# Third block's attention: query and key parts split on GpSimd, a running sum of the chunks, one total a group

## The chip, the cores and the metric

One core of a Trainium2 chip runs the whole program. The metric is device time in microseconds: the median of the timed runs. The engines are TensorE (PE in the profile; PEld are its weight loads), VectorE (DVE), ScalarE (ACT), GpSimd (POOL) and SyncE (SP), which here only issues DMAs. Each engine works through its own list of instructions in order; semaphores tie the lists together.

## The reference

Four transformer-like blocks run one after the other. The change touches the attention of the third:

```python
def _L2_xattn_ref(x, latents, attention_mask, ...):      # x: 64 context rows, latents: 512 rows, batch 4
    h = jnp.concatenate([x, latents], axis=1)            # 576 keys
    q = (latents @ q_w + q_b).reshape(b, k_len, NH, DH)  # 16 heads of 32
    kv = (h @ kv_w + kv_b).reshape(b, p + k_len, NH, DH, 2)
    kmat, v = (kv[..., 0], kv[..., 1])
    attn = jnp.einsum('bkhd,bnhd->bhkn', q, kmat) / DH
    attn = jnp.where(full_mask[:, None, None, :], attn, -jnp.inf)
    attn = jax.nn.softmax(attn.astype(jnp.float32), axis=-1).astype(q.dtype)
    attn_out = jnp.einsum('bhkn,bnhd->bkhd', attn, v).reshape(b, k_len, H)
    attn_out = attn_out @ out_w + out_b + residual
```

## The kernel before

`l2_attention_stage` handles 16 groups (`ALL`), each four heads of one of four batches; `turns(g)` is true for the second group of a batch but the last. Five chunks of keys (`CHUNKS`: four of 128 and one of 64 context keys) make up the 576.

For a group, TensorE projects the queries (`project_q`, four blocks of 512 columns) and keys (`project_k`, eight of 288). ScalarE copies them out with their bias (`take_projections`). VectorE splits each value into a rounded high part and the rest (`split`, two casts and two subtracts), so that logits can be computed in the fast float32r format. SP copies the parts with 24 DMAs into a stacked operand of each head (`load_stack`: `q_stack`, `k_stack`, six DMAs a head, double buffered over groups; a mask row goes first in the first two groups of a batch). TensorE then computes plain logits for 16 tiles (`logits`, four heads by four row blocks, each as two matmuls of 288 columns into `slot`), VectorE takes their row maximum (`maximum`, L1250), and four tiles of maxima are turned (`turn_tops`) and copied by ScalarE into the stack (`take_tops`). Now the turned logits (`logits_across`, L1093, keys on partitions) come out with the maximum already subtracted; ScalarE takes their exponential into `weighed`, a ring of three chunks (`exps`, L1204). `mix` multiplies the chunk with the values; ones matmuls (L1112, L1115) add the chunks up into `totals`. GpSimd adds chunks 0 and 1, and 2 and 3, so that TensorE needs one total of each pair and one of chunk 4. VectorE divides (`normalise`: reciprocal L1264, then a product) and, at the end of a batch, the output is projected (`project_out`, L1057).

The groups are staggered by hand. TensorE's list for group g holds, for chunks 0 to 3 and heads 0 to 3, a turned product of g and a logits tile of g+1 (a "step" below, numbered 0 to 15), with a mix of the previous chunk behind every four; then the last chunk's four products with the query projection of g+3 between them, the turning of the maxima of g+1, the last mixes and totals, and the key projection of g+3. After a batch's last group come the values of the next batch and the output projection. In its loop VectorE takes 16 maxima of g+1, normalises g, then splits g+3; SP loads the stack of g+2 as soon as the turned products of g are done with its buffer. A logits tile may run two ahead of its maximum, a turned product two ahead of its exponential.

## Time and profile before

| what | value |
|---|---|
| median of 3 runs | 3097.59 us (3094.41 to 3097.8) |
| the profiled execution | 3090.94 us, its span 3089.1 us |
| PE busy in the span | 2789.1 us (90%) |
| PE weight loads | 1982.5 us (64%) |
| DVE busy | 1472.4 us (48%) |
| ACT busy | 839.5 us (27%) |
| POOL busy | 349.2 us (11%) |
| the third block's attention | from 1354.2 us to about 2022 us |
| GpSimd's pair adds in it (L986) | 32, 145.5 us |
| the maxima (L1250) | 256, 183.1 us |
| the exponentials (L1204) | 320, 184.5 us |

Busy times are shares of the whole span, over stages with different limits; what an edit is worth here is read from the stretch of this attention alone. A matmul record's end is modelled, since matmuls are pipelined: the distance between starts tells more than the duration. A time in brackets is how long the engine was idle before the row, with what released it. The profile leaves the block's digit out of buffer names: `l_slot` is this stage's `l2_slot`. A matmul of plain float32 is recorded as two, one of float32r as one.

### The profile page before, as it was taken

The page shows a single profiled execution, that of the slowest core. Times are in us where ns is not written, and L with a number is a line of the kernel's source. Part 1 is how long each engine was busy: PE and PEld are TensorE (multiplying, and loading weights), DVE is VectorE, ACT ScalarE, POOL GpSimd, SP SyncE. Part 2 cuts the span into 40 slices and gives each one's busy share as a digit, 9 for nine tenths or more (in the row PEclk, how much of TensorE's full clock was granted, in tenths as well). Part 3 has the DMA queues.
Part 4 walks back from the last instruction along what each step waited for, and adds up shares of the span by engine and source line. Part 5 has one row for each costly group of instructions (what it writes and reads, how often), then busy time and mean ns, then how long its engine had stood idle before and what let it go on. Part 6 is the DMA issues. An engine that isn't in the chain of part 4 may idle for free. (4 is left out here: it accounts for less than half of the span.)

```text
span 3089.1 us, 30932 instructions
## 1 busy us (share of the span) xinstructions
PE 2789.1 (90%) x11800; PEld 1982.5 (64%) x11800; DVE 1472.4 (48%) x2117; ACT 839.5 (27%) x1580; POOL 349.2 (11%) x178
## 2 busy tenths in 40 slices
PE   6999979999969999988999999869999788779999
PEld 4777656777758888744445454348888544468887
DVE  3564474455575343135545454455343545374443
ACT  4233314332331111213435242431111122241110
POOL 2000002000012000012313122312000300040000
PEclk9999989999979999978999999879999899989999
DMA  3111011101010000202121211130000101110001
GB/s 121 55 55 54 1 60 56 55 1 55 0 60 28 14 14 1 109 23 49 44 58 44 57 44 53 27 126 28 14 14 1 62 28 62 45 61 28 28 0 55
DMA packets 60095, 130.64 MB, mean 42 GB/s; under 512 B 30673, under 2 KB 30802, under 8 KB 49234
## 3 DMA queue, kind: packets, MB, share of 16 engines
q1 hardware_dynamic: 43218, 128.61, 12.3%
q10 hardware_dynamic: 16768, 0.53, 0.3%
q8 instruction: 74, 1.21, 0.2%
q14 instruction: 35, 0.29, 0.0%
HBM read 83.03 MB, written 8.45 MB: 30 GB/s over the span
## 5 line engine op out<-in xcount | busy, mean ns | idle before, releaser
L1204 ACT ACTIVATE l_weighed<-l_across 128x512 f32<-128x512 f32 (+1 forms) x320 | 184.5, 595 | 245.8 <-PE l_across L1093 240.8
L1250 DVE TENSOR_REDUCE l_top<-l_slot 128x1 f32<-128x576 f32 x256 | 183.1, 753 | 51.7 <-PE l_slot L1076 46.9
L986 POOL TENSOR_TENSOR l_paired<-l_weighed 128x2048 f32<-128x2048 f32 x32 | 145.5, 4546 | 464.8 <-ACT l_weighed L1204 380.9
L1076 PE MATMUL l_slot<-l_k_stack,l_q_stack 97*128 97x288 f32 x512 | 140.1, 361 | 34.2 <-DVE l_top L1250 20.9
L1093 PE MATMUL l_across<-l_q_stack,l_k_stack 99*128 99x512 f32 (+1 forms) x320 | 165.9, 522 | 3.9 <-ACT l_weighed L1204 3.7
L1076 PEld LDWEIGHTS l_slot<-l_k_stack,l_q_stack 97*128 97x128 f32 x512 | 100.8, 220 | 78.7 <-DVE l_top L1250 48.4
L1264 DVE RECIPROCAL l_inverse<-l_totals 128x512 f32<-128x512 f32 x16 | 53.7, 3357 | 158.6 <-PE l_totals L1115 158.6
L475 PE MATMUL l0b_wide<-l0b_key_map,l0b_norm 128*128 128x260 f32 x512 | 118.7, 385 | 9.3 <-DVE l0b_soft L630 7.2
L475 PE MATMUL l0a_wide<-l0a_key_map,l0a_norm 128*128 128x260 f32 x512 | 118.7, 385 | 9.3 <-DVE l0a_soft L630 7.2
L1755 ACT ACTIVATE l2m_hidden<-l2m_up,columns 128x512 f32<-128x512 f32 x64 | 44.2, 691 | 270.5 <-PE l2m_up L131 264.3
L1755 ACT ACTIVATE l0m_hidden<-l0m_up,columns 128x512 f32<-128x512 f32 x64 | 44.1, 691 | 269.7 <-PE l0m_up L131 262.6
L1755 ACT ACTIVATE l3m_hidden<-l3m_up,columns 128x512 f32<-128x512 f32 x64 | 44.1, 691 | 268.9 <-PE l3m_up L131 261.8
L475 PEld LDWEIGHTS l0b_wide<-l0b_key_map,l0b_norm 128*128 128x128 f32 x512 | 95.6, 190 | 27.6 <-DVE l0b_soft L630 9.8
L475 PEld LDWEIGHTS l0a_wide<-l0a_key_map,l0a_norm 128*128 128x128 f32 x512 | 95.6, 190 | 27.6 <-DVE l0a_soft L630 9.8
L1093 PEld LDWEIGHTS l_across<-l_q_stack,l_k_stack 99*128 99x128 f32 (+1 forms) x320 | 63.1, 199 | 73.8 <-issue 35.9
L129 PE MATMUL l0m_up<-l0m_norm_hi,l0m_w1h 128*128 128x512 f32 x256 | 101.6, 397 | 0.7 <-POOL l0m_w1l L1662 0.7
L129 PE MATMUL l3m_up<-l3m_norm_hi,l3m_w1h 128*128 128x512 f32 x256 | 101.0, 395 | 1.1 <-POOL l3m_w1l L1662 0.7
L129 PE MATMUL l2m_up<-l2m_norm_hi,l2m_w1h 128*128 128x512 f32 x256 | 101.2, 395 | 0.7 <-POOL l2m_w1l L1662 0.7
L130 PE MATMUL l0m_up<-l0m_norm_lo,l0m_w1h 128*128 128x512 f32 x256 | 101.0, 395 | 0.0
L131 PE MATMUL l0m_up<-l0m_norm_hi,l0m_w1l 128*128 128x512 f32 x256 | 100.6, 393 | 0.0
L130 PE MATMUL l2m_up<-l2m_norm_lo,l2m_w1h 128*128 128x512 f32 x256 | 100.6, 393 | 0.0
L131 PE MATMUL l2m_up<-l2m_norm_hi,l2m_w1l 128*128 128x512 f32 x256 | 100.5, 392 | 0.0
(391 smaller groups left out, 6240.9 us busy)
## 6 DMA issues: line engine op xcount, KB each, us to landing
l_k_stack<-l_k_parts SPq DMA_DIRECT2D x192, 72.0 KB, 2.0
l_q_stack<-l_q_parts SPq DMA_DIRECT2D x192, 64.0 KB, 2.0
l0m_raw<-in_weights SPq DMA_DIRECT2D x8, 1024.0 KB, 4.8
l2m_raw<-in_weights SPq DMA_DIRECT2D x8, 1024.0 KB, 6.4
l3m_raw<-in_weights SPq DMA_DIRECT2D x8, 1024.0 KB, 4.8
x<-in_x SPq DMA_DIRECT2D x4, 1024.0 KB, 8.9
l0a_wk<-in_weights SPq DMA_DIRECT2D x4, 1024.0 KB, 5.4
l0a_wv<-in_weights SPq DMA_DIRECT2D x4, 1024.0 KB, 7.3
```

Source lines behind the costliest of these rows:

```text
L129: pe.matmul(out, lh, rh, start=start, stop=False)
L130: pe.matmul(out, lh, rl, start=False, stop=False)
L131: return pe.matmul(out, ll, rh, start=False, stop=stop)
L475: last = pe.matmul(wide[:, j, 0:W], norm[:, k, at:at + P], key_map[:, k, b, :, :].rearrange("p h c -> p (h c)"), start=k == 0, stop=k == K ...
L986: pool.tensor_tensor(paired[:, :, :], weighed[:, first % RING, :, :], weighed[:, (first + 1) % RING, :, :], ALU.add)\
L1076: last = pe.matmul(slot[:, 2 * (i % 2) + half, 0:HALF], q_stack[0:ROW + 1, g % 2, j, t * P:(t + 1) * P], k_stack[0:ROW + 1, g % 2, j, half ...
L1093: pe.matmul(across[0:height(c), use % 2, :], k_stack[0:LAST, g % 2, j, keys_of(c)], q_stack[0:LAST, g % 2, j, :], start=True, stop=True).t ...
L1204: act.activation(weighed[0:height(c), (CHUNKS * g + c) % RING, j, :], across[0:height(c), use % 2, :], ACT.Exp)\
L1250: dve.tensor_reduce(top[:, i % TPB, i // TPB:i // TPB + 1], slot[:, 2 * (i % 2):2 * (i % 2) + 2, 0:HALF], AX.XY, ALU.max, negate=True).the ...
L1264: dve.reciprocal(inverse[:, :], totals[:, :]).then_inc(s["inverse_ready"], 1)
L1755: act.activation(hidden[:, i % 2, :], up[:, m, :], activation, bias=n.col(bias, f * KT + m))\
```

## The change

- The logits tile is one matmul of 512 columns; the 64 context columns of a head's four row blocks go as four short matmuls into a bank of their own (`ctx_slot`), with one maximum for all four (`ctx_top`), and `split_tops` first takes the smaller of the two negated maxima.
- The key projection is split into `project_k0` (512 columns) and `project_k1` (64). All blocks of `project_q`, `project_k0` and `project_k1` of group g+3 are dealt out between the steps by a table (`EXTRA`) and share one new bank, `work`. ScalarE's copies move in between its exponentials.
- From group 2 on, the split of g+2 runs on GpSimd, between its second and third add of group g; the parts have one buffer instead of two, and `projected` two instead of one.
- GpSimd keeps a running sum of all five chunks (`add_chunk`, four adds a group). TensorE has one `total` a group, in the next group behind its chunk 0, and for a batch's last group behind the next batch's values. The exponentials wait for the adds that read their buffer.
- The reciprocal is cut into four quarters (`invert`), taken with the product at places 5 to 9 of the next group's maxima, or behind the values at the end of a batch.
- The turning of the next batch's input (`turn_next`) moves to the steps of chunk 0; mixes 0 and 1 stand together behind chunk 2's steps.

```diff
+        VALUE_BANK = (0, 1, 2, 0, 1)
+        OUT_BANK = (2, 0, 1, 2)
+        EXTRA = (((0, 1, 2, 3), (6, 7, 8, 9), (13, 14, 16, 17)), ((4, 5, 6, 7), (9, 10, 11, 12), (16, 17, 18, 19)))
+
+        def bank_of(g, piece):
+
+            if g == 0:
+                return (work[:, :], slot_bank[0], slot_bank[1])[piece]
+            if g == 1:
+                return (slot_bank[2], work[:, :], slot_bank[0])[piece]
+            return work[:, :]
...
+            def add_chunk(g, c):
+                at, tall = CHUNKS * g + c, height(c)
+                pool.wait_ge(s["across_read"], across_use(g, c, 3) + 1)
+                if c == 1 and g:
+                    pool.wait_ge(s["totals_done"], g)
+                if c > 1:
+                    pool.wait_ge(s["chunk_summed"], (CHUNKS - 1) * g + c - 1)
+                so_far = summed[0:tall, :, :] if c > 1 else weighed[0:tall, (at - 1) % RING, :, :]
+                pool.tensor_tensor(summed[0:tall, :, :], so_far, weighed[0:tall, at % RING, :, :], ALU.add)\
+                    .then_inc(s["chunk_summed"], 1)
+
+            def split(g):
+                q, k = projected[:, g % 2, 0, 0:S], projected[:, g % 2, 1, :]
+                pool.wait_ge(s["k1_out"], g + 1)
+                for j in range(4):
+                    pool.wait_ge(stack_loaded[(g - 1) % 2][j], loaded(g - 1))
+                pool.tensor_copy(q_parts[:, 0, :], q)
+                pool.tensor_copy(k_parts[:, 0, :], k).then_inc(s["parts_high"], 1)
+                pool.wait_ge(s["parts_high"], g + 1)
+                pool.tensor_tensor(q_parts[:, 1, :], q, q_parts[:, 0, :].bitcast(F32), ALU.subtract)
+                pool.tensor_tensor(k_parts[:, 1, :], k, k_parts[:, 0, :].bitcast(F32), ALU.subtract).then_inc(s["parts_ready"], 1)
 
             for g in range(ALL):
                 b = g // GROUPS
-                add_pair(g, 0)
+                add_chunk(g, 1)
+                add_chunk(g, 2)
+                if g + 2 < ALL:
+                    split(g + 2)
                 if turns(g):
-                    pool.wait_ge(s["k_done"], GROUPS * (b + 1))
+                    pool.wait_ge(s["k1_done"], GROUPS * (b + 1))
                     pool.tensor_copy(source[:, :, S:KEYS], n.ctx_f[:, :, (b + 1) * C:(b + 2) * C]).then_inc(s["ctx_ready"], 1)
-                add_pair(g, 1)
+                add_chunk(g, 3)
+                add_chunk(g, 4)
...
+            def project_extra(g, step):
+                at_q, at_k0, at_k1 = EXTRA[g >= 3 and turns(g - 3)]
+                if step in at_q:
+                    project_q(g, (at_q.index(step),))
+                if step in at_k0:
+                    project_k0(g, (at_k0.index(step),))
+                if step in at_k1:
+                    project_k1(g, (at_k1.index(step),))
...
-                for half in range(2):
-                    last = pe.matmul(slot[:, 2 * (i % 2) + half, 0:HALF], q_stack[0:ROW + 1, g % 2, j, t * P:(t + 1) * P],
-                                     k_stack[0:ROW + 1, g % 2, j, half * HALF:(half + 1) * HALF], start=True, stop=True)
-                last.then_inc(s["logits_done"], 1)
+                pe.matmul(slot[:, i % 2, :], q_stack[0:ROW + 1, g % 2, j, t * P:(t + 1) * P],
+                          k_stack[0:ROW + 1, g % 2, j, 0:S], start=True, stop=True).then_inc(s["logits_done"], 1)
+                if t == 2:
+                    pe.wait_ge(s["ctx_top_ready"], 4 * g + j)
+                    for u in range(TPB):
+                        last = pe.matmul(ctx_slot[:, u, 0:C], q_stack[0:ROW + 1, g % 2, j, u * P:(u + 1) * P],
+                                         k_stack[0:ROW + 1, g % 2, j, S:KEYS], start=True, stop=True)
+                    last.then_inc(s["ctx_logits_done"], 1)
...
+                last.then_inc(s["mix_done"], 1)
+
+            def total(g):
+                pe.wait_ge(s["chunk_summed"], (CHUNKS - 1) * (g + 1))
+                if g:
+                    pe.wait_ge(s["inverse_ready"], 4 * g)
+                for j in range(4):
+                    last = pe.matmul(totals[32 * j:32 * j + 32, :], ones[:, :], summed[:, j, :], start=True, stop=True)
+                last.then_inc(s["totals_done"], 1)
...
             for g in range(ALL):
-                m, b = g % GROUPS, g // GROUPS
                 for c in range(TPB):
                     for j in range(4):
                         logits_across(g, c, j)
                         if g + 1 < ALL:
                             logits(g + 1, TPB * c + j)
-                    if turns(g):
-                        turn_next(g, c)
-                    if c:
-                        mix(g, c - 1)
-                if g + 3 < ALL:
-                    pe.wait_ge(s["top_ready"], TILES_OF * (g + 2))
+                        if g + 3 < ALL:
+                            project_extra(g + 3, TPB * c + j)
+                        if turns(g) and c == 0:
+                            turn_next(g, j)
+                    if c == 0 and g % GROUPS:
+                        total(g - 1)
+                    if c == 2:
+                        mix(g, 0)
+                        mix(g, 1)
+                    if c == 3:
+                        mix(g, 2)
                 for j in range(4):
                     logits_across(g, TPB, j)
                     if g + 3 < ALL:
-                        project_q(g + 3, (j,))
+                        project_extra(g + 3, TILES_OF + j)
                 if g + 1 < ALL:
                     turn_tops(g + 1)
-                mix(g, CHUNKS - 2)
-                mix(g, CHUNKS - 1)
-                if g + 3 < ALL:
-                    project_k(g + 3)
-                if m == GROUPS - 1:
-                    if b + 1 < B:
-                        project_values(b + 1, g + 3)
-                    project_out(b)
+                mix(g, 3)
+                mix(g, 4)
+                if g % GROUPS == GROUPS - 1:
+                    if g + 1 < ALL:
+                        project_values(g // GROUPS + 1)
+                    total(g)
+                    project_out(g // GROUPS)
...
             def exps(g, c):
                 if CHUNKS * g + c >= RING:
                     act.wait_ge(s["mix_done"], CHUNKS * g + c - RING + 1)
-                if c == 3 or c == 4:
-                    act.wait_ge(s["pair_summed"], 2 * g + 1)
+                if c >= 3:
+                    act.wait_ge(s["chunk_summed"], (CHUNKS - 1) * g + 1)
                 elif g:
-                    act.wait_ge(s["pair_summed"], 2 * g)
+                    act.wait_ge(s["chunk_summed"], (CHUNKS - 1) * (g - 1) + c + 2)
                 for j in range(4):
                     use = across_use(g, c, j)
                     act.wait_ge(s["across_done"], use + 1)
                     act.activation(weighed[0:height(c), (CHUNKS * g + c) % RING, j, :], across[0:height(c), use % 2, :], ACT.Exp)\
                         .then_inc(s["across_read"], 1)
+                    if turns(g) and c == 0:
+                        take_next(g, j)
...
             for g in range(ALL):
                 for c in range(CHUNKS):
                     exps(g, c)
-                    if turns(g) and c < KT:
-                        take_next(g, c)
+                    if g + 3 < ALL and c == (1 if turns(g) else 0):
+                        take_q(g + 3)
+                    if g + 3 < ALL and c == (3 if turns(g) else 2):
+                        take_k0(g + 3)
                 if g + 1 < ALL:
                     take_tops(g + 1)
                 if g + 3 < ALL:
-                    take_projections(g + 3)
+                    take_k1(g + 3)
...
+                dve.tensor_reduce(top[:, t, j:j + 1], slot[:, i % 2, :], AX.X, ALU.max, negate=True).then_inc(s["top_ready"], 1)
+                if t == TPB - 1:
+                    dve.wait_ge(s["ctx_logits_done"], 4 * g + j + 1)
+                    dve.tensor_reduce(ctx_top[:, :, j], ctx_slot[:, :, 0:C], AX.X, ALU.max, negate=True).then_inc(s["ctx_top_ready"], 1)
...
+            def invert(g, quarter):
+                here = slice(quarter * P, (quarter + 1) * P)
+                if quarter == 0:
+                    dve.wait_ge(s["totals_done"], g + 1)
+                dve.reciprocal(inverse[:, here], totals[:, here]).then_inc(s["inverse_ready"], 1)
...
             for g in range(ALL):
                 m, b = g % GROUPS, g // GROUPS
+                late = g % GROUPS != 0
+                for i in range(TILES_OF):
+                    if g + 1 < ALL:
+                        maximum(g + 1, i)
+                    if late and i in (5, 6, 7, 8):
+                        invert(g - 1, i - 5)
+                    if late and i == 9:
+                        normalise(g - 1)
                 if g + 1 < ALL:
-                    for i in range(TILES_OF):
-                        maximum(g + 1, i)
                     split_tops(g + 1)
-                normalise(g)
-                if g + 3 < ALL:
-                    split(g + 3)
                 if m == GROUPS - 1:
                     if b + 1 < B:
                         take_values(b + 1)
+                    for quarter in range(4):
+                        invert(g, quarter)
+                    normalise(g)
                     add_out(b)
```

## Rows read from the trace of the kernel before

**Rows 1.** busy us of PE, PEld, DVE, ACT, POOL (instructions); then granted clock

```profile
1424.90:2021.90 597.00, 555.87 (x2494) 279.03 (x2492) 291.99 (x389) 244.02 (x419) 166.22 (x51) 0.94 0.18 45
...
1646.20:1678.10 31.90, 29.63 (x145) 16.34 (x145) 18.07 (x25) 15.23 (x27) 9.10 (x2) 0.89 0.22 53
```

**Rows 2.** TensorE in order of time: start, us, operation; first logits of a group

```profile
1426.33 0.51 PE L1076 MATMUL l_slot<-l_k_stack,l_q_stack 97*128 97x288 f32 x2 [0.83 <-ACT l_projected L1184]
...
1584.79 0.50 PE L1076 MATMUL l_slot<-l_k_stack,l_q_stack 97*128 97x288 f32 x2 [0.75 <-DVE l_rows L1274]
...
1613.54 0.51 PE L1076 MATMUL l_slot<-l_k_stack,l_q_stack 97*128 97x288 f32 x2 [0.80 <-ACT l_projected L1184]
...
1646.19 0.51 PE L1076 MATMUL l_slot<-l_k_stack,l_q_stack 97*128 97x288 f32 x2 [0.80 <-ACT l_projected L1184]
...
1678.07 0.51 PE L1076 MATMUL l_slot<-l_k_stack,l_q_stack 97*128 97x288 f32 x2 [0.81 <-ACT l_projected L1184]
...
1740.26 0.51 PE L1076 MATMUL l_slot<-l_k_stack,l_q_stack 97*128 97x288 f32 x2 [0.75 <-DVE l_rows L1274]
...
1899.02 0.49 PE L1076 MATMUL l_slot<-l_k_stack,l_q_stack 97*128 97x288 f32 x2 [0.75 <-DVE l_rows L1274]
```

**Rows 3.** TensorE in order of time, behind the start of a group

```profile
1648.88 0.85 PE L1076 MATMUL l_slot<-l_k_stack,l_q_stack 97*128 97x288 f32 x2 [1.45 <-DVE l_top L1250]
...
1649.52 0.63 PE L1093 MATMUL l_across<-l_q_stack,l_k_stack 99*128 99x512 f32 x1
...
1650.43 0.63 PE L1093 MATMUL l_across<-l_q_stack,l_k_stack 99*128 99x512 f32 x1
```

**Rows 4.** TensorE in order of time, at full clock

```profile
1629.68 0.60 PE L1014 MATMUL l_across<-ident,x 128*128 128x128 f32 x4
...
1637.03 2.06 PE L1105 MATMUL l_gathered<-l_weighed,l_values 128*32 128x512 f32 x16
...
1639.02 1.06 PE L1112 MATMUL l_totals<-l_paired,l_ones 128*32 128x512 f32 x8
...
1686.98 0.43 PE L1076 MATMUL l_slot<-l_k_stack,l_q_stack 97*128 97x288 f32 x2
...
1687.25 0.40 PE L1093 MATMUL l_across<-l_q_stack,l_k_stack 99*128 99x512 f32 x1
...
1687.49 0.43 PE L1076 MATMUL l_slot<-l_k_stack,l_q_stack 97*128 97x288 f32 x2
```

**Rows 5.** groups by form, 1354 to 2024: count, busy us, mean ns, idle before

```profile
L1250 DVE TENSOR_REDUCE l_top<-l_slot 128x1 f32<-128x576 f32 x256 | 183.1, 753 | 51.7 <-PE l_slot L1076 46.9
...
L1204 ACT ACTIVATE l_weighed<-l_across 128x512 f32<-128x512 f32 x256 | 147.4, 596 | 194.4 <-PE l_across L1093 189.6
...
L986 POOL TENSOR_TENSOR l_paired<-l_weighed 128x2048 f32<-128x2048 f32 x32 | 145.5, 4546 | 464.8 <-ACT l_weighed L1204 380.9 <-PE l_totals L1112 83.9
...
L1264 DVE RECIPROCAL l_inverse<-l_totals 128x512 f32<-128x512 f32 x16 | 53.7, 3357 | 158.6 <-PE l_totals L1115 158.6
```

**Rows 6.** groups by form on GpSimd, the whole span: a cast

```profile
L1660 POOL CAST l3m_w1h<-l3m_raw 128x2048 fp32r<-128x2048 f32 x1 | 1.9, 1889 | 241.9 <-DMA l3m_raw<-in_weights 241.9
```

**Rows 7.** SP in order of time: first and sixth load of a stack

```profile
1446.79 0.51 SPq L947 DMA_DIRECT2D l_q_stack<-l_q_parts  x1
...
1449.87 0.59 SPq L948 DMA_DIRECT2D l_k_stack<-l_k_parts  x1
```

**Rows 8.** TensorE in order of time: first values, last output projection

```profile
1381.01 17.47 PE L1047 MATMUL l_slot<-l_wv,l_source 128*128 128x512 f32 x40
...
2004.27 16.88 PE L1057 MATMUL l_slot<-l_wo,l_mixed 128*128 128x512 f32 x32 [4.21 <-DVE l_mixed L1268]
```

**Rows 9.** page, part 6: DMA issues, KB each, us to landing

```profile
l_k_stack<-l_k_parts SPq DMA_DIRECT2D x192, 72.0 KB, 2.0
```

**Rows 10.** TensorE in order of time: the first turned product of the loop

```profile
1424.88 0.61 PE L1093 MATMUL l_across<-l_q_stack,l_k_stack 99*128 99x512 f32 x1
```

202 lines of the change are left out of this document (103 added, 99 removed).

## The prediction, made before the changed kernel ran

> **What bounds the kernel now.** Only the third block's attention changes, so I first read the stretches: its loop lasts 597.0 us, TensorE is busy for 555.87 of them at a mean granted clock of 0.94, VectorE for 291.99, ScalarE for 244.02, GpSimd for 166.22 [rows 1]. TensorE sets the pace, and a saving has to shorten its queue or its waits. Next I read TensorE's order of time at the first logits product of each group, which gives the periods [rows 2]. In the second batch they are 28.75, 32.65, 31.88 and 62.19 us (the last holds the batch's values and output projections), 155.5 in all; three batches, from 1426.33 to 1899.02, take 472.7. Then I looked at a group's start: two waits, 0.80 for ScalarE's projection and 1.45 for VectorE, which is dividing, multiplying and splitting [rows 2, 3]. Behind them the same pair of products repeats every 0.91 us [rows 3] where elsewhere it repeats every 0.51 [rows 4]; that stretch has a mean granted clock of 0.89 [rows 1]. So a wait of 2.2 us also costs a few us at 1.2 GHz. Last I read the price of each engine's instructions [rows 5, 6].
>
> **Prices.** A step (one turned-logits product of 512 columns, one logits tile) is 0.51 us [rows 4]. A projection block of 512 columns is 0.86 (17.47 / 20, a little less for the tail) [rows 8]. Four matmuls of a mix or of a total take 1.0 (2.06 for two mixes, 1.06 for one total) [rows 4]. An exponential is 0.60 [rows 5]. A 576-wide maximum is 0.715 (183.1 / 256) [rows 5], so one of 512 about 0.65 and the new 256-wide one for the context keys about 0.38, both scaled estimates. A GpSimd add of 2048 columns is 4.55 [rows 5].
>
> **TensorE's work, per group.** Removed: two of three totals, 2.0 us. The logits keep their columns (512 + 64 for 2 x 288), but the 64 context columns become four short products a head. No row has that shape. Bounds: the nearest short one, four 128-column transposes, 0.60 [rows 4], against 0.24 each for a whole 512-column product [rows 4], 1.0; below, 0.1, since the 64 columns themselves were paid before. I take 0.5 a head, 2.0 a group, because the transposes are nearest. The key projection becomes 4 x 0.86 plus four 64-column blocks at 0.1 to 0.5, taken 0.3: 4.6 against 4 x 576 / 512 x 0.86 = 3.9, so 0.7 more. Net: 0.7 us more work than before. The gain can only come from waits: projections are now dealt out between the steps, where VectorE and ScalarE limited the pace, and VectorE's division moves into the next group in four quarters of about 0.84 (3.357 / 4 [rows 5]), placed at steps 5 to 8, beside 0.86 blocks. I cost that at nothing; if these blocks did not stand there, it would be 2 us.
>
> **The new loop, from which the sum follows.** GpSimd's queue for a group is now add 1, add 2, split of group g+2, add 3, add 4. Busy: 4 x 4.55 plus the split. The split is two casts of 1088 columns together (1.889 / 2048 a column, 1.0 [rows 6]) and two subtracts (at the add's rate, 2.4), with four starts and a hand-over 3.8: 22.0 a group, under every period. But the split stands behind add 2, and add 2 waits for the exponentials of chunk 2. The stacks' loads stand behind the split on SP's queue, and TensorE stands behind the first head's six loads when it reaches the next group's first logits. From TensorE's start of step 11 (last of chunk 2): exponential over 1.2, add 2 4.55, split 3.8, hand-overs 0.3, six loads: the sixth issues 3.1 after the first [rows 7] and lands 2.0 later [rows 9]. Sum 15.0, with 0.6 more where the mask's load goes first (one group start in a batch). The split also waits for the stack before it to be whole, since the parts have one buffer now: 24 loads at 0.62, 17 us after that stack's first issue, which is some 10 us before it is due. The context copy and, in group 0, the four adds of `rows` stand behind the split and cost the loop nothing; they come out of GpSimd's spare time. Before, that split ran on VectorE nearly a group earlier, and the loads waited only for the stack's buffer.
> TensorE's own way from step 11 to that place: rest of the step 0.5, mixes 0 and 1 2.0, steps 12 to 15 with two small blocks 3.1, mix 2 1.0, four last products at ScalarE's pace 2.4, drain 0.3, turning the maxima 0.6, then four copies into the stack, 2.4, estimated at one exponential each, with 0.2 around them (mixes 3 and 4, 2.0, run beside). Sum 12.5. So it waits 2.5 us more, and idle 3.0 together. A wait of that size is like those in rows 3, so I add half clock behind it: 5 us of it in steps that TensorE alone limits lose 2.5.
>
> **Periods after, from first logits to first logits.** Group 0 of a batch, no wait before it: steps 0 to 3 4 x (0.51 + 0.86) + 0.5, steps 4 to 10 7 x 0.51 + 4 x 0.86 + 1.0, ScalarE's pace 0.3, less the 0.3 ahead of the first logits: 14.0, plus 15.0 = 29.0 (before 28.75). Group 1 (it turns the next batch's input, 0.6 four times, and has its query blocks later): 4.9 + total 1.0 + 9.7 - 0.3 + clock 2.5 = 17.8, plus 15.0 = 32.8 (before 32.65). Group 2: 14.0 + 1.0 + 2.5 = 17.5, plus 15.6 = 33.1 (before 31.88). Group 3: 17.5, then no loop but the batch's end: 11.6 to the last mix, values 17.2, total 1.0, and now a bare wait. The total stands behind the values, so the output projection waits for four quarter divisions and the product, 4.4; before, VectorE did this beside the values. The one place of the trace with that wait is the end: 4.21 idle, then 32 matmuls in 16.88 instead of 13.8 [rows 8]. So 11.6 + 17.2 + 1.0 + 4.4 + 16.9 + 0.3 = 51.4, and 68.9 in all (before 62.19). A batch: 163.8; three: 491.4 against 472.7, **+18.7**.
> Start: the third group's projections (3.4 + 3.9) now run inside VectorE's 16 maxima; two 64-column key projections (1.2) and a later copy (0.4) come in: **-5.7** before the first turned product, now at 1424.88 [rows 10].
> End: before, 122.1 from 1899.02 to TensorE's end at 2021.15 [rows 2, 8]. After: 29.0; a group without projections 12.1 + 15.0; 12.1 to the last step 11. The final group has no logits, so GpSimd's adds bound it: exponentials of its chunk 1 done 18.8 later, four adds 18.2, total 1.0, division 4.4, projection 16.9: 59.3. Sum 127.5, **+5**.
> Total +18.0: the profiled execution (span 3089.1, 3090.94 with what lies around it) would take 3109; it was 6.6 below the median of the shown runs, 3097.59, on which I put the same +18: **3115 us**. About 0.2%, 6 us, is what a measurement of this kernel can tell from no change.
>
> **A rule weighed.** The trace's adds take 4.52 to 4.58 us beside VectorE's maxima, which read PSUM (mean 4546 ns over 32 [rows 5]): no contention. The Trainium skill (SBUF - State Buffer, "SBUF: two separate sides") says that GpSimd and a VectorE instruction with two SBUF inputs exclude each other for a whole instruction, and no run here shows it. By it the two small maxima operations of each group would wait for a subtract of the split, at most 1.4 us each; most of that lies under the 2.5 us wait, so the sum would stay at 3115, and the first rival would lose some 10 us of its gain.
>
> **Rivals.** (1) *The loop closes in time, and TensorE's own work sets the period.* It happens if the way over GpSimd and SP is under 12.5 us, or TensorE's own way is nearer to 15. For it: the difference is 2.5 in 15, and several prices are estimates. Against it: 4.55, 3.1 and 2.0 are measured [rows 5, 7, 9]. Worth 11 starts x 2.5, 3 x 0.6 and nine spells of half clock x 2.5: 52 us, 3063, faster. If only the clock stays up, 22.5 less: 3092, faster too. (2) *The short context products cost what long ones do*, 1.0 a head; three of four heads lie outside the loop: 1.5 x 16 = 24 more, 3139. (3) *Chunk adds are late for the exponentials* (chunk 1 of the next group waits for add 3): add 4 ends 9.1 after the split, 3.8 after the first logits, and the exponentials that need it come after eight steps, so this would need 5 us more on GpSimd; then each group gains those, 3150.
>
> **How the numbers follow.** Forecast as worked out, 3098 to 3130: 0.52. Rival 1 whole or in part, 3060 to 3092: 0.33. Rival 2: 0.11. Rival 3: 0.04. Of the forecast's own spread some 0.10 falls within 6 us of the median, 0.02 below; from rival 1 0.02 is within. So faster 0.33, same 0.12, slower 0.55. The range leaves out the far ends of rivals 1 and 3: 3064 to 3139.
>
> **What would show it.** The split's last instruction about 9.6 us behind step 11; the first logits of groups 1, 2 and 3 of a batch waiting for a load of the stacks, about 3 us idle, with steps at half pace behind; output projections with some 4.4 us idle ahead of each; a period of 33 for group 2. Wrong if these logits follow the copies of the maxima at once, if the clock stays up there, or if the logits pair takes over 0.7 us with nothing beside it.

## The result and the profile after

The changed kernel takes **3145.53 us** (median of 4 runs, 3139.01 to 3147.32) against 3097.7 for the kernel before beside it: ratio 1.0145 [1.0127, 1.0163], slower by 48 us between the medians. The forecast was 3115 with a range up to 3139; the sign was right, the size was not. The profiled execution has a span of 3145.5 us (before 3089.1), so the two traces differ by 8 us more than the medians; those 8 lie ahead of the stage, whose first instruction starts at 1362.36 instead of 1354.21, and it moves by as much between executions (from 1354.1 to 1365.3 in the kernels below, whose edits stand behind it). From that first instruction to TensorE's last output projection the stage takes 715.9 us instead of 666.9: 48.9 of loss.

The first lines of the page of the changed kernel (columns as before):

```profile
span 3145.5 us, 30676 instructions
PE 2805.5 (89%) x11544; PEld 1985.9 (63%) x11544; DVE 1484.0 (47%) x2189; ACT 842.1 (27%) x1598; POOL 551.1 (18%) x266
PEclk9999979999979999989999998679999899989999
```

The digits 8, 6, 7 of the clock line (its 25th to 27th slice of 78.6 us each) are this stage's end. Next the stretches, with the columns of [rows 1]; the changed kernel from the first logits of the first batch to those of the last, then from there to TensorE's end:

```profile
1431.64:1928.70 497.06, 445.36 (x1801) 224.04 (x1800) 236.88 (x363) 190.89 (x337) 279.12 (x111) 0.92 0.18 45
1928.70:2078.22 149.52, 120.50 (x435) 54.12 (x435) 70.49 (x92) 53.19 (x94) 84.96 (x28) 0.71 0.11 30
```

and the same two stretches of the kernel before:

```profile
1426.33:1899.02 472.69, 448.07 (x1993) 230.68 (x1993) 235.59 (x319) 189.97 (x325) 124.91 (x39) 0.95 0.19 48
1899.02:2021.15 122.13, 107.20 (x499) 48.17 (x499) 55.45 (x69) 53.02 (x93) 41.31 (x12) 0.92 0.14 37
```

In what follows *the batches* is the first of these stretches (the periods of the first three batches) and *the end* the second. The batches lose 24.4 us and all of it is idle time of TensorE (51.7 instead of 24.6, with 2.7 less work). The end loses 27.4: TensorE has 64 matmuls fewer and yet 13.3 us more of busy time, at a mean granted clock of 0.71 instead of 0.92, and 14.1 us more of waits. GpSimd's busy time has more than doubled in both. TensorE's waits by operation tell where they stand (groups on TensorE over the loop of the changed kernel; the idle time before them and what ended it come last):

```profile
L1156 PE MATMUL l_across<-l_q_stack,l_k_stack 99*128 99x512 f32 (+1 forms) x320 | 195.8, 619 | 13.2 <-ACT l_weighed L1274 6.4 <-ACT l_q_stack L1261 5.5
L1134 PE MATMUL l_slot<-l_k_stack,l_q_stack 97*128 97x512 f32 x256 | 117.7, 460 | 23.2 <-DMA l_k_stack<-l_k_parts 17.7 <-DVE l_rows L1358 2.3 <-DVE l_top L1324 2.2
L1117 PE MATMUL l_ctx_slot<-l_wo,l_mixed 128*128 128x512 f32 x64 | 37.2, 735 | 17.6 <-DVE l_mixed L1352 17.6
L1177 PE MATMUL l_totals<-l_summed,l_ones 128*32 128x512 f32 x128 | 21.4, 747 | 5.8 <-POOL l_summed L1002 5.8
L1080 PE MATMUL l_work<-l_source,l_wk 128*128 128x64 f32 x112 | 20.2, 264 | 5.5 <-POOL l_source L1024 5.5
L1149 PE MATMUL l_across<-ident,l_top_parts 128*128 128x128 f32 x64 | 12.7, 332 | 21.1 <-DVE l_top_parts L1338 20.8 <-ACT l_weighed L1274 0.3
```

Against these, the kernel before waits like this:

```profile
L1076 PE MATMUL l_slot<-l_k_stack,l_q_stack 97*128 97x288 f32 x490 | 132.1, 356 | 31.2 <-DVE l_top L1250 19.0 <-ACT l_projected L1184 8.9 <-DVE l_rows L1274 2.3
L1057 PE MATMUL l_slot<-l_wo,l_mixed 128*128 128x512 f32 x128 | 58.9, 620 | 4.2 <-DVE l_mixed L1268 4.2
L1086 PE MATMUL l_across<-ident,l_top_parts 128*128 128x128 f32 x64 | 10.1, 283 | 2.0 <-DVE l_top_parts L1259 1.4 <-ACT l_weighed L1204 0.6
```

The waits that the change was made for did go: before its logits TensorE waited 19.0 us for the maxima and 8.9 for ScalarE's projections, and now 2.2 for the maxima. What came in their place is more. The wait for loads (17.7) and the one ahead of the output projections (17.6) were forecast. The largest was not: **21.1 us ahead of the turning of the maxima**, for an operation of VectorE on 16 columns, where it was 2.0. Half of it, 10.4, stands in the last two groups.

VectorE and GpSimd in order of time at the last two groups of the changed kernel show what that is (start, duration, engine, operation):

```profile
1981.20 0.88 DVE L1332 TENSOR_TENSOR l_top<-l_top,l_ctx_top 128x16 f32<-128x16 f32 x1
1982.12 4.44 DVE L1336 CAST l_top_parts<-l_top 128x16 fp32r<-128x16 f32 x1
1986.59 0.19 DVE L1338 TENSOR_TENSOR l_top_parts<-l_top,l_top_parts 128x16 f32<-128x16 f32 x1
...
1980.64 1.41 POOL L1014 TENSOR_TENSOR l_k_parts<-l_projected,l_k_parts 128x576 fp32r<-128x576 f32 x1
1982.01 9.16 POOL L1002 TENSOR_TENSOR l_summed<-l_summed,l_weighed 128x2048 f32<-128x2048 f32 x2
...
2015.59 3.87 DVE L1332 TENSOR_TENSOR l_top<-l_top,l_ctx_top 128x16 f32<-128x16 f32 x1
2019.49 0.18 DVE L1336 CAST l_top_parts<-l_top 128x16 fp32r<-128x16 f32 x1
2019.71 4.39 DVE L1338 TENSOR_TENSOR l_top_parts<-l_top,l_top_parts 128x16 f32<-128x16 f32 x1
...
2014.89 9.16 POOL L1002 TENSOR_TENSOR l_summed<-l_summed,l_weighed 128x2048 f32<-128x2048 f32 x2 [2.14 <-ACT l_weighed L1274]
```

A cast of 16 columns takes 4.44 us, a subtract 4.39, where either takes 0.18 when nothing of GpSimd's stands beside it. Each drawn-out one (*held*, in what follows) ends where a GpSimd instruction ends: 2015.59 + 3.87 = 2019.46, and the first of the two adds is over at about 2014.89 + 9.16 / 2 = 2019.47 (half of the pair; instruction by instruction, the trace has each held operation end 30 to 51 ns behind the GpSimd instruction beside it). Between the two adds one VectorE operation gets through, and the next waits for the whole second add. That is the exclusion that the prediction weighed from the Trainium skill (SBUF - State Buffer, "SBUF: two separate sides"), which counts VectorE's two-port copies to it beside operations with two SBUF inputs; the trace agrees for the minimum and the subtract, which have two such inputs, and it has the cast held as well (4.44 us), though no run shows in which mode that cast ran. The prediction priced it at most at 1.4 us a wait, as if only the split's subtracts could stand beside these operations. The maxima, which read PSUM, are not held: 680 ns in the mean for 512 columns, and 679 in the run below where GpSimd's adds are one column a head wide. The adds themselves keep 4.5 us.

### The profile page after: what moved, and what is told of

Its sections match the earlier page's. It is cut to its first block and busy times, and to the rows that moved or that the text cites. A ratio compares the mean times of both kernels' runs of the same rounds, so it can differ in the third digit from the quotient of the medians.

```text
span 3145.5 us, 30676 instructions
## 1 busy us (share of the span) xinstructions
PE 2805.5 (89%) x11544; PEld 1985.9 (63%) x11544; DVE 1484.0 (47%) x2189; ACT 842.1 (27%) x1598; POOL 551.1 (18%) x266
## 5 line engine op out<-in xcount | busy, mean ns | idle before, releaser
L1324 DVE TENSOR_REDUCE l_top<-l_slot 128x1 f32<-128x512 f32 x256 | 171.0, 680 | 203.5 <-PE l_slot L1134 202.9
L1002 POOL TENSOR_TENSOR l_summed<-l_summed,l_weighed 128x2048 f32<-128x2048 f32 (+1 forms) x48 | 217.6, 4534 | 11.2 <-ACT l_weighed L1274 8.3
L1156 PE MATMUL l_across<-l_q_stack,l_k_stack 99*128 99x512 f32 (+1 forms) x320 | 195.8, 619 | 13.2 <-ACT l_weighed L1274 6.4
L1134 PE MATMUL l_slot<-l_k_stack,l_q_stack 97*128 97x512 f32 x256 | 117.7, 460 | 23.2 <-DMA l_k_stack<-l_k_parts 17.7
L1156 PEld LDWEIGHTS l_across<-l_q_stack,l_k_stack 99*128 99x128 f32 (+1 forms) x320 | 63.6, 200 | 115.1 <-issue 53.1
L1002 POOL TENSOR_TENSOR l_summed<-l_weighed 128x2048 f32<-128x2048 f32 x16 | 72.9, 4557 | 304.2 <-ACT l_weighed L1274 304.2
L130 PE MATMUL l3m_up<-l3m_norm_lo,l3m_w1h 128*128 128x512 f32 x256 | 99.9, 390 | 0.0
L131 PE MATMUL l3m_up<-l3m_norm_hi,l3m_w1l 128*128 128x512 f32 x256 | 99.9, 390 | 0.0
```

Source lines behind the costliest of these rows:

```text
L130: pe.matmul(out, lh, rl, start=False, stop=False)
L131: return pe.matmul(out, ll, rh, start=False, stop=stop)
L1002: pool.tensor_tensor(summed[0:tall, :, :], so_far, weighed[0:tall, at % RING, :, :], ALU.add)\
L1134: pe.matmul(slot[:, i % 2, :], q_stack[0:ROW + 1, g % 2, j, t * P:(t + 1) * P], k_stack[0:ROW + 1, g % 2, j, 0:S], start=True, stop=True). ...
L1156: pe.matmul(across[0:height(c), use % 2, :], k_stack[0:LAST, g % 2, j, keys_of(c)], q_stack[0:LAST, g % 2, j, :], start=True, stop=True).t ...
L1324: dve.tensor_reduce(top[:, t, j:j + 1], slot[:, i % 2, :], AX.X, ALU.max, negate=True).then_inc(s["top_ready"], 1)
```

## The experiments

Edits are against the changed kernel unless said otherwise. Beside them the kernel before took 3098.8 to 3101.0 us; measured times are medians.

**Is it the exclusion?** GpSimd waits until VectorE has split the maxima before it starts its third add:

```diff
+                if g + 1 < ALL:
+                    pool.wait_ge(s["top_split"], g + 2)
                 add_chunk(g, 3)
```

> Changed kernel, with one wait more: GpSimd's third add waits until VectorE has split the maxima. Theory exclusion (a GpSimd instruction on SBUF holds up VectorE's three small SBUF operations until it ends, so that turning the maxima of the last two groups comes 3.7 and 6.7 us late): those two idle times go, the 4.4 us records of L1336 and L1338 vanish, 8 to 15 us less than the changed kernel's 3145.5, so 3130 to 3138. The 1.2 to 1.3 us ones stay, since they stand behind the split. Rival, GpSimd's adds themselves bound the end of the stage: holding them back makes the end later, 3145 to 3155.

Measured 3135.58 us (1.0109 [1.0084, 1.0135]), 10 less. In the last two groups the cast is back from 4437 to 185 ns and the subtract from 4393 to 189; the period in which the first stands goes from 34.91 to 31.14 us. In the groups before, the cast and the subtract still stand beside the split's subtracts and take 1.2 to 1.3 us each, and the batches stay at 497.2 us. All of the gain is in the end: 139.4 us for 149.5. Not all of it is the held operations, though. The mean granted clock of the end is 0.78 now, against 0.71; and in the runs of two other edits below, which change nothing in the last groups and leave the held operations there at 3.9 to 4.4 us, the end took 142.8 us at 0.82 (the total among the values) and 141.2 at 0.79 (the query blocks first). What set the clock so low in the changed kernel, no run shows.

The opposite edit lets the split run before add 2, which brings the parts 4.9 us sooner but lays add 2 beside the small operations:

```diff
                 add_chunk(g, 1)
-                add_chunk(g, 2)
                 if g + 2 < ALL:
                     split(g + 2)
+                add_chunk(g, 2)
```

> Changed kernel with GpSimd's split of the next but one group ahead of the second add instead of behind it. Theory queue alone (the loads stand behind the split, which stands behind add 2): parts are ready 4.5 us sooner, then only the stack's buffer holds the loads, first logits 14.0 us after step 11 instead of 15.4: 11 starts x 1.3, 3130. Theory exclusion: the small operations of the maxima now fall into adds of 4.55 us, L1332, L1336 or L1338 take up to 4.5 us in every group, turning starts 9.3 or 13.8 us after step 11; with 13.8 the first logits come 17 us after it and the kernel takes 3155 to 3175.

Measured 3169.13 us (1.0224 [1.0199, 1.025]), slower by another 24 and inside the range of the exclusion's theory. The parts are ready 4.7 us behind step 11 instead of 9.65, yet the turning of the maxima comes 14.0 behind it. Nearly every group pays, as VectorE's groups by form show (count, busy us, mean ns):

```profile
L1338 DVE TENSOR_TENSOR l_top_parts<-l_top,l_top_parts 128x16 f32<-128x16 f32 x16 | 66.3, 4143 | 0.6
L1332 DVE TENSOR_TENSOR l_top<-l_top,l_ctx_top 128x16 f32<-128x16 f32 x16 | 36.2, 2264 | 1.7
```

So GpSimd's queue alone, without the exclusion, is refuted: that theory had this kernel faster. The same happens when only the context copy is put ahead of add 1, so that the third add starts sooner and meets VectorE's subtract:

> Changed kernel with GpSimd's copy of the next batch's context ahead of the first add instead of behind the split. Theory: TensorE's small key projection of the second group of a batch waits for this copy (1.84 us idle, three times), and all behind it in that group is late: turning at 9.8 instead of 12.4 us after step 11, first logits at 15.4 instead of 17.6: 3 x 2.2 = 7 us less, 3139. Rival: the way over the split and the loads hides it, no change, 3145.

Measured 3142.87 (1.013 [1.0103, 1.0156]). TensorE's wait of 1.84 us for that copy goes, and in the same groups the subtract takes 4426 ns; the 2.7 us between the medians are within what two such measurements can tell.

**All of it together**: split before add 2, wait for `top_split` before add 2, copy first.

> Changed kernel with three moves on GpSimd: the context copy first, the split ahead of the second add, and behind the split a wait until VectorE has split the maxima. So no SBUF instruction of GpSimd stands beside VectorE's small ones. Theory exclusion plus queue: L1332, L1336 and L1338 all at 0.2 us, turning 9 us after step 11, first logits 14.0 us after it (the stack's buffer holds the loads now): against the changed kernel's 3145.5, 11 x 1.4 for the logits, 10 for the end as in the run with the wait alone, 7 for the copy: 3113. Rival: if moving the split sooner was bad in itself (3169 before), it stays above 3145.

Measured 3138.95 (1.0103 [1.0074, 1.0132]), where much more was expected. The small operations take 175 to 190 ns everywhere and the maxima turn at 9.0 us behind step 11, but the next first logits come at 13.9 to 15.0 where nothing is turned, hardly sooner than in the changed kernel (14.8 to 15.8). The batches are 9.9 us shorter (487.2), and the held-back adds make the end 2.3 longer (151.9), where the wait alone had made it 10 shorter.

**What holds the next group, if not the split?** GpSimd's adds are cut to one column each. This kernel leaves out most of the sum, so its output is not the reference's; all else runs as before.

```diff
-                so_far = summed[0:tall, :, :] if c > 1 else weighed[0:tall, (at - 1) % RING, :, :]
-                pool.tensor_tensor(summed[0:tall, :, :], so_far, weighed[0:tall, at % RING, :, :], ALU.add)
+                so_far = summed[0:tall, :, 0:1] if c > 1 else weighed[0:tall, (at - 1) % RING, :, 0:1]
+                pool.tensor_tensor(summed[0:tall, :, 0:1], so_far, weighed[0:tall, at % RING, :, 0:1], ALU.add)
```

> Changed kernel with GpSimd's adds cut to one column a head (the sums of the weights are left out, so the output isn't the reference's); order and waits stay. It prices GpSimd's 18 us a group as a whole. Theory: first logits 14.0 us after step 11 (11 x 1.4), no late maxima or total in the last groups (10 + 10), copy in time (7): 3103. What stays is TensorE's own work and the wait at a batch's end. Rival, TensorE's way alone sets the period and GpSimd hardly matters: 3135 or more.

Measured 3108.69 us (1.0019 [1.0001, 1.0036]): GpSimd's adds cost 37 us in all, 24 of them behind the last batch's first logits (125.8 us to TensorE's end instead of 149.5). The split is over 5.3 us behind step 11, and the next first logits still come 14.0 to 15.2 behind it. So there the floor is not the split; TensorE still waits 21.0 us for loads. What it is, SyncE's queue shows in the run of the pairs below (SyncE's DMA issues and TensorE in order of time):

```profile
1640.93 0.51 SPq L960 DMA_DIRECT2D l_q_stack<-l_q_parts  x1
1641.48 0.59 SPq L961 DMA_DIRECT2D l_k_stack<-l_k_parts  x1
...
1640.40 0.45 PE L1151 MATMUL l_across<-l_q_stack,l_k_stack 99*64 99x512 f32 x1
1640.68 0.33 PE L1075 MATMUL l_work<-l_source,l_wk 128*128 128x64 f32 x2
1641.13 0.63 PE L1144 MATMUL l_across<-ident,l_top_parts 128*128 128x128 f32 x4
1641.69 2.06 PE L1163 MATMUL l_gathered<-l_weighed,l_values 128*32 128x512 f32 x16
1643.68 1.06 PE L1168 MATMUL l_totals<-l_summed,l_ones 128*32 128x512 f32 x8
1644.67 1.06 PE L1171 MATMUL l_totals<-l_weighed,l_ones 64*32 64x512 f32 x8
...
1647.15 0.50 PE L1129 MATMUL l_slot<-l_k_stack,l_q_stack 97*128 97x512 f32 x1 [0.99 <-DMA l_k_stack<-l_k_parts]
```

The loads start when the group's last turned product frees the stack's buffer, and the logits can start 6.2 us later. Before the change more stood in that place on TensorE (first load of a stack, then TensorE):

```profile
1668.47 0.53 SPq L947 DMA_DIRECT2D l_q_stack<-l_q_parts  x1
...
1668.92 2.06 PE L1105 MATMUL l_gathered<-l_weighed,l_values 128*32 128x512 f32 x16
1670.90 1.07 PE L1112 MATMUL l_totals<-l_paired,l_ones 128*32 128x512 f32 x8
1671.90 1.06 PE L1115 MATMUL l_totals<-l_weighed,l_ones 64*32 64x512 f32 x8
1672.89 4.15 PE L1034 MATMUL l_slot<-l_source,l_wk 128*128 128x288 f32 x16
```

The eight key blocks (4.15 us), the two totals and the end of the last query block kept TensorE at work until its next logits at 1678.07, 9.6 us behind the first of these loads, and in that kernel none waited for a load. The change deals the projections out over the steps and so uncovers the loads. What is left as cover are the mixes 3 and 4, and in the run of the pairs two totals.

**The batch's end.** Total and division of a batch's last group among the next batch's values: `total` behind the third chunk of the values, two quarters behind the third and two behind the fourth copy of the values on VectorE.

> Changed kernel with the total of a batch's last group behind the third of the five value chunks instead of behind all, and the quarters of the division between VectorE's copies of the values. Forecast's own term (a bare wait of 4.3 us ahead of three output projections, and half clock behind it, 2.9): 3 x 7.2 = 22 us less than the changed kernel, 3124. Rival (the clock there costs nothing, or falls for another reason): 3 x 4.3 = 13, 3132. No change would mean that something else is late there.

Measured 3118.02 (1.0057 [1.0035, 1.0079]), 27.5 less. The three periods with a batch's end go from 70.0, 69.3 and 70.0 us to 63.6, 63.3 and 64.0: 18.3 us together, between the rival's 13 and the 22 of the forecast's term. Another 6.7 are in the end (142.8 for 149.5), where the edit changes nothing and the mean granted clock was 0.82 for 0.71; so the 27.5 must not be put down to the division alone. In order of time on TensorE, the changed kernel and then this one:

```profile
1575.06 1.07 PE L1177 MATMUL l_totals<-l_summed,l_ones 128*32 128x512 f32 x8
1580.44 2.08 PE L1117 MATMUL l_ctx_slot<-l_wo,l_mixed 128*128 128x512 f32 x2 [4.31 <-DVE l_mixed L1352]
```

```profile
1575.70 3.70 PE L1119 MATMUL l_ctx_slot<-l_wo,l_mixed 128*128 128x512 f32 x8
1579.24 7.03 PE L1119 MATMUL l_slot<-l_wo,l_mixed 128*128 128x512 f32 x16
```

The first two matmuls behind the bare wait take 2.08 us, eight without it 3.70: the granted clock is 0.50, the lower of the two levels, in the 4 us behind the wait, and 0.98 in the 12.5 behind those. The one place before with such a wait was slower in the same way [rows 8].

**The split back on VectorE**, behind `split_tops`:

> Changed kernel with the split of group g+2 on VectorE, right behind the split of the maxima, as the only part undone. Without exclusion it would be done 9 us after step 11, as on GpSimd: 3145. Theory exclusion: the maxima's small operations and the split's four now stand against adds 3 and 4, turning at 14 to 15 us, parts at 17 or later, first logits at 22 or later, 11 x 7: 3200 to 3240.

Measured 3254.12 (1.0492 [1.047, 1.0514]), above even the range of the exclusion's theory. VectorE's groups by form:

```profile
L1325 DVE TENSOR_TENSOR l_top_parts<-l_top,l_top_parts 128x16 f32<-128x16 f32 x16 | 70.9, 4434 | 0.6
L1319 DVE TENSOR_TENSOR l_top<-l_top,l_ctx_top 128x16 f32<-128x16 f32 x16 | 58.2, 3640 | 1.7
L1300 DVE TENSOR_TENSOR l_k_parts<-l_projected,l_k_parts 128x576 fp32r<-128x576 f32 x16 | 16.3, 1019 | 0.0
```

Without the split between them GpSimd's adds follow each other all through the small operations, and the split itself comes late. The parts are ready 17.5 to 21.8 us behind step 11. So, with the running sum in place, the split is better on GpSimd; the two runs of the pairs below keep it there.

**Covering the loads with query blocks.** The query blocks of g+3 stand ahead of the group's first step, where the loads land, and ScalarE takes the last key piece ahead of the maxima.

> Changed kernel with the four query blocks of group g+3 in one piece ahead of group g's first step (not in the groups that turn the next input), so TensorE has 3.4 us of work while the stack's loads land, and ScalarE's small key copy ahead of the copies of the maxima. Theory: the wait before the first logits of groups 2 and 3 of a batch is idle time that work can fill, and its half clock goes with it: 6 starts x (2.5 + 2.5) = 30 less than the changed kernel's 3145.5, 3115. Rival (the loads' time only moves on to steps that VectorE limits, and the clock falls anyway): 6 x 1 or less, 3140.

Measured 3135.55 (1.0106 [1.008, 1.0132]), a gain of 10, nearer to the rival of 3140, and even this is not the covering: TensorE's wait for loads falls from 17.7 to 9.9 us, but the batches take 496.9 us as they did (497.1), and the gain is in the end, where the edit moves nothing. On top of the other edits it gave nothing. Four combinations stand here together: all of split sooner, wait before add 2, copy first and total among the values (the first); that with the stacks' loads released head by head (the second); with the query blocks first (the third); with both (the fourth).

> The three moves of the kernel with copy first, split sooner and wait, and with them the total among the values, as measured alone (27 us). Sum: 3113 - 27 = 3086, faster than the kernel before (3098 to 3101). If the two don't add up, because the clock stays low anyway, 3095 to 3105.

> The combined kernel (3122.6 measured) with the load of each head's stack released by that head's own last turned product, 1.8 us sooner for head 0. Theory: the stack's buffer now holds the first logits at 14.0 us after step 11; it becomes 12.5: 11 x 1.5 = 16 less, 3106; if the shorter wait keeps the clock up, 20 more, 3086. Rival, another thing is late at once (the copies of the maxima): under 5 less.

> The combined kernel (3122.6) with the query blocks ahead of the first step. Theory: 6 starts x (2 + 2.5) = 27 less, 3096, about the kernel before. Rival: 3117.

> Both: query blocks first and loads released head by head. Theory: waits at group starts gone but for the group that turns the next input: 3085, faster than the kernel before (3098 to 3101) by 0.5 per cent. Rival: the clock falls in the steps whatever stands before them, 3105.

Measured 3122.64 (1.0065 [1.0042, 1.0087]), 3123.81 (1.0072 [1.0048, 1.0095]), 3126.97 (1.0082 [1.0057, 1.0106]) and 3131.52 (1.0097 [1.0071, 1.0123]): none as fast as the total among the values alone. The first shows what the held-back adds are worth: its batches take 470.2 us where the total among the values alone has 478.9, its end 151.8 where that has 142.8. Holding the adds back costs in the end what it gains in the batches.

The second tests the floor. With the loads released head by head the first logits come 12.4 to 13.4 us behind step 11 (13.9 to 15.2 in the first), so the release of the stack's buffer was indeed what held them. But the time does not fall, since another wait takes the place of the one for loads (TensorE's groups in the second):

```profile
L1140 PE MATMUL l_slot<-l_k_stack,l_q_stack 97*128 97x512 f32 x254 | 111.8, 441 | 8.1 <-DVE l_top L1336 3.5 <-DVE l_rows L1370 2.3 <-DMA l_k_stack<-l_k_parts 2.0
L1183 PE MATMUL l_totals<-l_summed,l_ones 128*32 128x512 f32 x128 | 26.1, 903 | 53.8 <-POOL l_summed L1004 53.8
```

Of loads TensorE waits 2.0 us (19.5 in the first), of the running sum 53.8 (23.7): `total` stands behind chunk 0 of the next group, and with its adds held back GpSimd is not done by then. The four adds a group are the next thing that is late.

**The end.** In the last three groups GpSimd adds nothing and TensorE adds the five chunks itself, in front of each mix:

```diff
+                if g >= DIRECT:
+                    for j in range(4):
+                        last = pe.matmul(totals[32 * j:32 * j + 32, :], ones[0:tall, :],
+                                         weighed[0:tall, (CHUNKS * g + c) % RING, j, :], start=c == 0, stop=c == CHUNKS - 1)
```

> Edit on the changed kernel, one thing alone: in the last three groups of the loop GpSimd adds no chunks; TensorE adds them itself, five totals of 1.0 us a group in front of the mixes (4 us more of TensorE's work a group). The result is the same. Theory (GpSimd's four adds a group, which have no later group to hide in, set the end of the stage): the last three groups, 34.9 + 86.0 = 120.9 us from the second-last first logits to TensorE's end, come to about 30 + 71 = 101, so the kernel to 3126. Rival (the end is long through the bare division and the output projection at half clock, 4.4 + 16.9, or through the waits on VectorE): TensorE's 8 to 12 us of more work eat what is won, 3143 to 3150.

Measured 3129.42 (1.0085 [1.0066, 1.0104]), 16 less although TensorE has 12 us more to do, against the 19.5 of the theory. The end goes from 149.5 to 136.3 us, and the same edit takes 13.0 from the end of the first and 13.7 from that of the second of the four combinations. On top of three of the other sets (the wait before the third add with the total among the values; then the first and the second of the four combinations):

> Three edits that each act on another term: GpSimd waits for the split of the maxima before its third add (alone -10), the total and the division of a batch's last group stand among the next batch's values (alone -27.5), and TensorE adds the chunks of the last three groups. The first and the third act on the same last groups, so together about -15 of the two. Theory: 3145.5 - 27.5 - 15 - 5 = 3098, level with the kernel before. Rival (the waits turn into others, as in the combinations run so far, of which no part added up): 3110 to 3118.

> The combination of the earlier split, the wait before add 2, the copy first and the total among the values (3122.6), and TensorE adds the chunks of the last three groups. Its loss against the kernel before lies almost all behind the last batch's second group in the trace: 214.5 us from the last batch end to TensorE's end against 185.8. Theory (GpSimd's adds at the end are what is left): 3122.6 - 22 = 3100. Rival (TensorE's added work and half clock keep it): 3113 to 3120.

> As the one before, and the stacks' loads are released head by head (alone no gain, 3123.8). TensorE waits 6.7, 6.4, 7.1 and 5.2 us for the sum in the last four groups of that kernel; the first three batches took 156.7 us against 155.5. Theory: 3123.8 - 22 = 3102. Rival: 3113 or more.

Measured 3111.78 (1.004 [1.0026, 1.0053]), 3106.35 (1.0014 [1.0001, 1.0027]) and 3109.9 (1.003 [1.0017, 1.0042]). The first came out 14 above its theory, inside the rival's range; the other two are 6 and 8 above theirs and 7 and 3 under their rivals'.

**The running sum undone, all else left as changed**: two pairs a group on GpSimd, three totals on TensorE.

```diff
-                add_chunk(g, 1)
-                add_chunk(g, 2)
+                add_pair(g, 0)
                 if g + 2 < ALL:
                     split(g + 2)
...
-                add_chunk(g, 3)
-                add_chunk(g, 4)
+                add_pair(g, 1)
...
+                if c in (2, 4):
+                    pe.wait_ge(s["chunk_summed"], 2 * g + c // 2)
+                    for j in range(4):
+                        last = pe.matmul(totals[32 * j:32 * j + 32, :], ones[:, :], summed[:, j, :], start=c == 2, stop=False)
```

> Edit on the changed kernel: the running sum alone is undone. GpSimd adds two pairs a group as before the change, TensorE has three totals a group again (2.0 us more work a group), split, projections, context product and the quarters of the division stay as changed. The result is the same. Theory (the running sum is what costs: GpSimd's adds before the split, beside the small VectorE operations and at the end): the split ends 4.5 us sooner, the small operations take 180 ns wherever no add stands beside them, the end of the stage loses some 20 us; against it 16 x 2.0 us of TensorE's work, of which 11 x 2 to 3 us fill waits. 3145.5 - 37 + 10 = 3118, of which the later division at a batch's ends (27) is what remains. Rival (the running sum pays for its cost with the totals that it saves, and the loss comes from the rest of the change): 3140 to 3150.

Measured **3100.6 us** (0.9996 [0.9983, 1.001]), level with the kernel before and 45 under the changed one; better than the 3118 of the theory. The small operations take 174 to 191 ns in all groups; the batches go from 497.1 to 476.5 us and the end from 149.5 to 128.5. The waits on TensorE for the loads and for the maxima are these (the two groups of the changed kernel, L1134 and L1149, above):

```profile
L1129 PE MATMUL l_slot<-l_k_stack,l_q_stack 97*128 97x512 f32 x253 | 108.7, 430 | 12.4 <-DMA l_k_stack<-l_k_parts 7.2 <-DVE l_top L1316 2.5 <-DVE l_rows L1350 2.2
L1144 PE MATMUL l_across<-ident,l_top_parts 128*128 128x128 f32 x64 | 10.3, 285 | 5.2 <-ACT l_weighed L1266 3.4 <-DVE l_top_parts L1330 1.4
```

17.7 us of waits for loads are 7.2 now, although the loads come no sooner (next first logits 15.5 us behind step 11 in either). The two totals that the running sum saves had stood just where TensorE waits for the loads: taken away there they were worth nothing, and the one total left, now among the steps, costs its 1.06. The run with adds of one column bears this out: GpSimd's adds are next to nothing there, and yet, with one total a group, TensorE waits 21.0 us for loads and the kernel takes some 8 us more than with the pairs.

**And the division at a batch's end among the next values**, as in the third experiment:

> As the one before, and at a batch's end VectorE divides among the next batch's values, which the earlier total allows. Theory: three batch ends x 8 to 9 us: 3118 - 26 = 3092, faster than the kernel before by a little. Rival: 3110 and more, if pairs and the dealt-out projections clash.

Measured **3074.73 us** (0.9918 [0.9898, 0.9937]): faster than both kernels, and than its theory. Its stretches, as above, batches and end:

```profile
1426.70:1878.20 451.50, 435.46 (x1993) 213.67 (x1992) 214.04 (x363) 189.65 (x337) 170.94 (x87) 1.00 0.20 50
1878.20:2007.53 129.33, 115.95 (x499) 49.69 (x499) 55.06 (x92) 53.38 (x94) 48.87 (x20) 0.85 0.13 35
```

The batches take 451.5 us against 472.7 before and 497.1 after, at a mean granted clock of 1.00: 25 less than with the pairs alone, nearly all of it in the three periods with a batch's end (60.6 us each, where the pairs alone have 68.0 to 70.2). The end is still 7 us longer than before; why was not tried.

## Why the prediction was wrong

The direction came as forecast; the size did not. Of the sum's terms the end (+5) failed most, with 22 of the 31 us by which the stage went over the sum; the batches (+18.7) make 5.7 of the rest and the start (-5.7) 3.7.

- **The end of the stage, "+5", is the step that failed most**: measured +27.4. Behind the first period (28.6, forecast 29.0) the next took 34.9 us and all that follows 86.0, where 27.1 and 71.4 were forecast. The final group was seen to be bound by GpSimd's adds, but not that the adds hold up VectorE's small operations in the two groups ahead of it, so that the maxima are turned 14.7 and 17.4 us behind step 11 instead of 9.3. And half clock was priced for the output projection alone: the two groups with the held operations ran at mean granted clocks of 0.60 and 0.59. The runs bound the parts: with adds of one column this stretch is 24 us shorter (125.8), with TensorE adding the chunks itself 13, with pairs 21; letting GpSimd wait is worth 10. How much of these is the wait itself and how much the clock that came with it stays open.
- **"Most of that lies under the 2.5 us wait" held in the batches and failed behind them.** The step priced the exclusion at 1.4 us a wait, from the split's subtracts, and at nothing in the sum. In the batches that is about what came: cast and subtract take 1.2 to 1.3 us each, but the maxima are turned only 0.7 us later for it (9.75 behind step 11 for 9.0), and the loads are later still. It forgot the adds, 4.5 us each, that follow the split directly: in the last two groups the operations are held 0.7 + 4.3 and 3.7 + 4.2 us.
- **Split and next first logits: the number was right, half the reason was not.** Forecast 9.6 and 15.0 us behind step 11; measured 9.65 and 14.8 to 15.8 where nothing is turned. But two paths end there at once. TensorE's own way, 12.5, was right too, as the run with loads released head by head shows (12.4 to 13.4); left out was that the loads wait for the last turned product, and so the runs with an early split show 14 to 15 all the same. So rival 1 in its full form, 3063, could not come true by a faster split, and the wait has a second cause: the projections that covered the loads were moved away.
- **"The context copy ... cost the loop nothing" failed.** TensorE waits 1.84 us for it in three groups, 5.5 us in all: the key blocks of 64 columns need it and it stands behind the split. With it the next first logits of group 1 come 17.4 us behind step 11 (second batch) instead of 15.0, and the period is 34.7 instead of the 32.8 forecast; group 2 and 3 came out at 30.5 and 69.3 (33.1 and 68.9), group 0 at 29.1 (29.0). The second batch's sum, 163.6 against 163.8, is right by errors that cancel, which is luck; the first takes 166.0 and the third 167.5. Three batches: +24.4, forecast +18.7.
- **The batch's end was right**: 4.31 us of bare wait (forecast 4.4) and half clock behind it, 68.9 forecast against 69.3 to 70.0. Moving the division away gives these three periods 18.3 us back, near the 3 x 6.7 by which they had been forecast over those before.
- **Start**: forecast -5.7, measured -2.0 (from the stage's first instruction to the first turned product, 68.7 where it was 70.7 [rows 10]). TensorE waits 1.44 us for the split maxima and 2.43 for ScalarE's copies there.
- **Prices**: the four context products start to start take 0.36 us and 0.53 as a record (forecast 0.5; rival 2 is out), a reciprocal's quarter 0.93 (0.84), a context maximum 0.42 (0.38), one of 512 columns 0.68 (0.65). GpSimd's two casts are 0.61 and 0.67, its subtracts 1.28 and 1.40, 3.95 us for the split in a row (3.8). Rival 3 did not come: ScalarE's only wait for an add is 0.84 us, in the last group. Where the adds are held back their lateness shows elsewhere, in TensorE's wait for the sum.
- **Totals saved, 2.0 us a group**, were entered at full price in TensorE's work. Undoing the running sum gives 45 us back, more than the 37 that making its adds one column wide does, since the totals taken away left waits.

Two wrong steps recur, then. The end was summed up without asking what the adds hold up where no later group hides it. And work was priced by its duration at the place it left, not by what it had covered there: so with the key blocks, and so with the totals.

## What to carry to other kernels

Before work goes to GpSimd, list VectorE's small operations on the critical path that read and write SBUF alone: each can wait for a whole GpSimd instruction (here up to 4.4 us), however short it is itself. When work is dealt out over a loop, name the transfer that it had covered and leave something in its place; work saved in a place where an engine waits anyway is worth nothing. Count the end of a stage by itself, since what overlaps the next group stands bare in the last.

## What the runs showed of the hardware

- A VectorE operation of 16 columns on SBUF takes 0.18 us alone and up to 4.44 us beside a GpSimd add of 2048 columns; it ends 30 to 51 ns behind the GpSimd instruction. It holds for the minimum and the subtract (two inputs) and for the cast (one input); VectorE's maxima, which read PSUM, are not held (680 ns beside wide adds, 679 with adds of one column), and GpSimd is not slowed (4534 and 4557 ns a group of adds against 4546 [rows 5]).
- Two adds of GpSimd in a row let one VectorE operation through between them, no more: 3.87, 0.18, 4.39 us in the lines above (the cast runs in the gap, the subtract meets the second add). Even one is not sure: in four groups of the run with the split on VectorE the subtract took 5.6 us, held over an add and the 1.25 us instruction behind it.
- The granted clock was lower where TensorE had waited, as in [rows 3]: over the last 149.5 us of the stage, with 29 us of waits, its mean was 0.71, and the kernel whose batches have the shortest waits (16.0 us) runs them at 1.00. But waits alone do not give the number: the same end with 31.6 us of waits had 0.82 in the run with the total among the values.
